# A second set of expert weight buffers, loaded a trip ahead, and a step's wait for the pieces of the bias

## The reference

```
def _L0_ffn_ref(x, ...):
    x = x + _msa(_layernorm(x, ln1_w, ln1_b), w_qkv, w_proj)     # softmax attention
    x = x + _moe_mlp(_layernorm(x, ln2_w, ln2_b), gate_w, gate_b, w1, w2)
    return x
# _moe_mlp: expert = argmax(x @ gate_w + gate_b) of 8, then gelu(x @ w1[expert]) @ w2[expert]
x = L0_attn_x
x = x + 0.5 * _L0_ffn_ref(_layernorm(x), ...)                    # stage 0
x = x + _L0_attn_ref(_layernorm(x), ..., rel_bias_table)         # stage 1, scores + relative bias
x = x + 0.5 * _L0_ffn_ref(_layernorm(x), ...)                    # stage 2
```

## Time and profile before

| | us |
|---|---|
| median of 3 runs | 2681.46 (2679.43 to 2685.08) |
| the profiled execution | 2694.05, span 2692.2 |
| PE busy | 2393.4 (89%) |
| ACT, DVE, POOL busy | 2023.6 (75%), 1966.4 (73%), 807.2 (30%) |
| mean granted clock of PE | 0.945 of full speed |
| DMA | 257.55 MB, 96 GB/s |
| copy of the turned tokens on ACT (L1182) | 0.67 each |
| the 24 matmuls of a trip's w1 product | 2.94 at full clock, 4.30 to 5.46 in the tail |
| mean granted clock in the trips of the tail | 0.77 to 0.80 |
| issues of two scatters in a row on POOL | 1.26 apart |
| POOL's gather of batch 2 in the tail, last issue | 2619.5 to 2621.0 |
| POOL's gather, first of the last eight | starts at 2672.32, eight end at 2686.8 |

### The profile page before, as it was taken

One profiled execution on the slowest core, in us unless ns is written; L12 is line 12 of the kernel. 1 busy time (PEld: TensorE's weight loads), 2 busy tenths in 40 slices (PEclk: granted clock), 3 DMA queues, 4 the chain that ended last, 5 costly groups with the idle time before them and its releaser, 6 DMA issues.

```text
span 2692.2 us, 63549 instructions
## 1 busy us (share of the span) xinstructions
PE 2393.4 (89%) x24940; PEld 947.9 (35%) x24940; DVE 1966.4 (73%) x3256; ACT 2023.6 (75%) x3724; POOL 807.2 (30%) x1087
## 2 busy tenths in 40 slices
PE   3899987888998999999999999999998998998824
PEld 1232323323533543443333333332223432533524
DVE  6988993687588579668888888898987697597000
ACT  1688875777788778777777777888988887888711
POOL 1353432443243151224333113114121033043051
PEclk7899998989999999999999999999999999999957
DMA  4333245534324542643533423211103304303324
GB/s 110 98 109 111 64 118 157 141 86 114 104 61 99 168 141 89 174 129 96 150 104 97 141 81 104 61 26 38 50 17 86 105 14 104 104 14 75 99 54 132
DMA packets 259826, 257.55 MB, mean 96 GB/s; under 512 B 48860, under 2 KB 216604, under 8 KB 255400
## 3 DMA queue, kind: packets, MB, share of 16 engines
q1 hardware_dynamic: 248264, 245.10, 31.5%
q0 software_dynamic: 11264, 8.40, 1.8%
HBM read 189.54 MB, written 76.15 MB: 99 GB/s over the span
## 4 chain that ended last, share of the span: by engine, by line
PE 54%; DVE 16%; ACT 7%; issue 7%; DMA 6%; SPq 6%; POOL 3%; POOLq 0%; DVEq 0%; ACTq 0%
PE psum L905 18%; DVE maxes L1209 12%; PE psum L832 10%; PE psum L867 8%; PE psum L888 4%; ACT probs L1092 4%; PE psum L1040 4%; DMA neg_max<-max_parts 3%; PE psum L1029 3%; PE psum L848 2%; SPq L468 2%; PE psum L956 2%; ACT L1092 2%; DMA q_staged<-neg_max 1%; DVE biased L1214 1%
## 5 line engine op out<-in xcount | busy, mean ns | idle before, releaser
L1092 ACT ACTIVATE probs<-psum 128x512 f32<-128x512 f32 x3072 | 1659.5, 598 | 320.3 <-PE psum L867 182.3
L1209 DVE TENSOR_REDUCE maxes<-psum 128x2 f32<-128x1024 f32 x1216 | 1435.4, 1218 | 394.6 <-PE psum L832 392.2
L905 PE MATMUL psum<-probs,v_ones 128*9 128x256 f32 (+1 forms) x11520 | 947.5, 401 | 0.0
L867 PE MATMUL psum<-q_staged,k_staged 51*128 51x512 bf16 (+1 forms) x3072 | 638.9, 384 | 62.5 <-ACT probs L1092 41.0
L832 PE MATMUL psum<-k_staged,q_staged 48*128 48x512 bf16 x3072 | 612.8, 395 | 78.9 <-DVE maxes L1209 50.0
L1214 DVE CUSTOM_DVE_ANT_0 biased<-psum,strips 128x512 bf16<-128x512 f32 x640 | 413.0, 687 | 113.7 <-PE psum L832 101.4
L644 POOL CAST max_parts<-max_turned 128x32 bf16<-128x32 f32 x96 | 20.1, 209 | 1318.9 <-DVE max_turned L1252 1318.9
L832 PEld LDWEIGHTS psum<-k_staged,q_staged 48*128 48x128 bf16 x3072 | 147.8, 93 | 725.2 <-DVE maxes L1209 364.2
L867 PEld LDWEIGHTS psum<-q_staged,k_staged 51*128 51x128 bf16 (+1 forms) x3072 | 258.5, 95 | 216.3 <-ACT probs L1092 96.6
L905 PEld LDWEIGHTS psum<-probs,v_ones 128*9 128x9 f32 x11520 | 171.1, 88 | 395.5 <-issue 282.5
L1029 PE MATMUL psum<-m_yt,m_w 128*128 128x128 f32 x960 | 133.7, 303 | 22.7 <-DMA m_w<-in_w 22.3
(11 more groups left out here) (143 smaller groups left out, 1571.7 us busy)
## 6 DMA issues: line engine op xcount, KB each, us to landing
m_w<-in_w SPq DMA_DIRECT2D x240, 256.0 KB, 3.4
near<-bias_near SPq DMA_DIRECT2D x16, 1920.0 KB, 9.7
q_staged<-q_parts SPq DMA_DIRECT2D x96, 192.0 KB
k_staged<-k_parts SPq DMA_DIRECT2D x96, 192.0 KB
strips<-bias_strips SPq DMA_DIRECT2D x16, 1152.0 KB, 5.6
q_parts<-p_part SPq DMA_DIRECT2D x24, 384.0 KB, 3.2
k_parts<-p_part SPq DMA_DIRECT2D x24, 384.0 KB, 3.8
bias_cuts<-bias_window SPq DMA_DIRECT2D x64, 120.0 KB
```

Source lines behind the costliest of these rows:

```text
L867: mm_ = pe.matmul(bank[:, :], k.kst[p][rows_, j // 2, kt * P:(kt + 1) * P], k.qst[p][rows_, j // 2, half * HALF:(half + 1) * HALF], start= ...
L905: last = pe.matmul(heads_bank[32 * j:32 * j + VC, columns], k.v[:, batch_of(u) * KT + kt, u % QUADS * 4 + j, :], probs[:, step % 3 * 4 + j ...
L1092: act.activation(probs[:, step % 3 * 4 + e % 4, :], bank[:, :], ACT.Exp).then_inc(taken, 1)
L1209: dve.reduce_max(maxes[u % 2][:, half, 2 * i:2 * i + 2, t, chunk], slot, AX.X).then_inc(drained, 1)
```

## The change

The weights get two sets of buffers, used by the parity of the trip's number over all sets, each with its own pair of semaphores. A load of a set of buffers waits for the trip two before, not for the last one. On SP, the weights of trips 0 and 1 of a set are loaded at `route_step` + 13 to + 16 (w1 of trip 0, w2 of trip 0, w1 of trip 1, w2 of trip 1, one a step), those of trip t + 2 in the steps after trip t's w1 product. The first tokens are loaded at the trip's step - 4 in place of - 2, which is a step ahead of the `carry_max`. The store of a trip's result now stands ahead of a w2 load. The room that the descriptors of POOL's DMAs get is set to 4096 bytes a partition. And in all steps in which pieces of the bias are handled, SP waits, before anything of `sp_between`, for the first score tile of that step.

```diff
@@ -258,7 +258,8 @@
     route_chain = k.sem("route_chain")
     scattered = [k.sem(f"scattered{p}") for p in range(2)]
     gathered = [k.sem(f"gathered{p}") for p in range(2)]
-    m_in, w1_in, w2_in, m_stored, finished = (k.sem(s) for s in ("m_in", "w1_in", "w2_in", "m_stored", "finished"))
+    m_in, m_stored, finished = (k.sem(s) for s in ("m_in", "m_stored", "finished"))
+    w1_in, w2_in = [k.sem(f"w1_in{p}") for p in range(2)], [k.sem(f"w2_in{p}") for p in range(2)]
 
 
     probs = k.sb("probs", [P, 3 * 4, HALF])
@@ -330,8 +331,8 @@
     numbers, upto = k.sb("tile_numbers", [P, MT]), k.sb("upto", [P, E * E])
     y = k.sb("m_y", [P, SLOTS, C])
     y_t = k.sb("m_yt", [P, SLOTS * P])
-    w1 = [k.sb(f"m_w1_{r}", [P, HID]) for r in range(SLOTS)]
-    w2 = [k.sb(f"m_w2_{r}", [P, 4, C]) for r in range(SLOTS)]
+    w1 = [[k.sb(f"m_w1_{p}_{r}", [P, HID]) for r in range(SLOTS)] for p in range(2)]
+    w2 = [[k.sb(f"m_w2_{p}_{r}", [P, 4, C]) for r in range(SLOTS)] for p in range(2)]
     hidden = [k.sb(f"m_hidden{r}", [P, HID]) for r in range(SLOTS)]
     expert_out = k.sb("m_out", [P, SLOTS, C])
 
@@ -356,6 +357,12 @@
 
     def batch_of(u):
         return u // QUADS % B
+
+    def trip_index(n, b, trip):
+        return set_index[n, b] * TRIPS + trip
+
+    def trip_key(done):
+        return (*SETS[done // TRIPS], done % TRIPS)
 
     def group_tiles(b, h):
         return slice(b * KT + h * 4, b * KT + h * 4 + 4)
@@ -539,25 +546,24 @@
 
     def load_w1(sp, n, b, trip):
 
-        at = set_index[n, b]
-        sp.wait_ge(routed, at + 1)
-        if at or trip:
-            before = (n, b, trip - 1) if trip else (*SETS[at - 1], TRIPS - 1)
-            sp.wait_ge(taken, seat[("m_hidden", *before, SLOTS - 1)] + 1)
+
+        done = trip_index(n, b, trip)
+        sp.wait_ge(routed, set_index[n, b] + 1)
+        if done >= 2:
+            sp.wait_ge(taken, seat[("m_hidden", *trip_key(done - 2), SLOTS - 1)] + 1)
         for r in range(SLOTS):
-            sp.dma_start(w1[r][:, :], w["ffn"]["w1"][bass.ds(expert_of(sp, n, b, trip, r), 1), :, :].rearrange(
-                "o p h -> p (o h)")).then_inc(w1_in, 16)
+            sp.dma_start(w1[done % 2][r][:, :], w["ffn"]["w1"][bass.ds(expert_of(sp, n, b, trip, r), 1), :, :].rearrange(
+                "o p h -> p (o h)")).then_inc(w1_in[done % 2], 16)
 
     def load_w2(sp, n, b, trip):
 
-        at = set_index[n, b]
-        sp.wait_ge(routed, at + 1)
-        if at or trip:
-            before = (n, b, trip - 1) if trip else (*SETS[at - 1], TRIPS - 1)
-            sp.wait_ge(taken, seat[("m_down", *before)] + 1)
+        done = trip_index(n, b, trip)
+        sp.wait_ge(routed, set_index[n, b] + 1)
+        if done >= 2:
+            sp.wait_ge(taken, seat[("m_down", *trip_key(done - 2))] + 1)
         for r in range(SLOTS):
-            sp.dma_start(w2[r][:, :, :], w["ffn"]["w2"][bass.ds(expert_of(sp, n, b, trip, r), 1), :, :].rearrange(
-                "o (q p) c -> p (o q) c", p=P)).then_inc(w2_in, 16)
+            sp.dma_start(w2[done % 2][r][:, :, :], w["ffn"]["w2"][bass.ds(expert_of(sp, n, b, trip, r), 1), :, :].rearrange(
+                "o (q p) c -> p (o q) c", p=P)).then_inc(w2_in[done % 2], 16)
 
     def store_tokens(sp, n, b, trip):
 
@@ -573,6 +579,9 @@
 
     def sp_between(sp, step):
 
+        cutting = any(-1 - CUT_LOADS <= step - s < 15 for s in NEAR_STEPS)
+        if cutting or step // 8 * len(QUIET) < QUADS * (CUTS + STRIP_CUTS):
+            sp.wait_ge(scored, seat["exp", step // UNIT_STEPS, step % UNIT_STEPS * 4] + 1)
         if step % 8 in QUIET:
             piece = step // 8 * len(QUIET) + QUIET.index(step % 8)
             if piece == 0:
@@ -594,18 +603,23 @@
                 store_parts(sp, n, b, h)
         for n, b in SETS:
             first = trip_step(n, b, 0)
-            if step == first - 2:
+            for trip in range(2):
+                if step == route_step(n, b) + 13 + 2 * trip:
+                    load_w1(sp, n, b, trip)
+                if step == route_step(n, b) + 14 + 2 * trip:
+                    load_w2(sp, n, b, trip)
+            if step == first - 4:
                 load_tokens(sp, n, b, 0)
-                load_w1(sp, n, b, 0)
-                load_w2(sp, n, b, 0)
             for trip in range(TRIPS):
-                if step == trip_step(n, b, trip) + 2 and trip + 1 < TRIPS:
-                    load_tokens(sp, n, b, trip + 1)
-                    load_w1(sp, n, b, trip + 1)
+                if step == trip_step(n, b, trip) + 2:
+                    if trip + 1 < TRIPS:
+                        load_tokens(sp, n, b, trip + 1)
+                    if trip + 2 < TRIPS:
+                        load_w1(sp, n, b, trip + 2)
                 if step == trip_step(n, b, trip) + 3:
-                    if trip + 1 < TRIPS:
-                        load_w2(sp, n, b, trip + 1)
                     store_tokens(sp, n, b, trip)
+                    if trip + 2 < TRIPS:
+                        load_w2(sp, n, b, trip + 2)
         for b in range(B):
             if step == gather_step(2, b) + 4:
                 store_batch(sp, b)
@@ -1021,23 +1035,23 @@
 
     def pe_hidden(pe, n, b, trip, r):
 
-        bank = open_bank(pe, "m_hidden", n, b, trip, r)
+        bank, done = open_bank(pe, "m_hidden", n, b, trip, r), trip_index(n, b, trip)
         if r == 0:
             pe.wait_ge(taken, seat["m_turn", n, b, trip] + 1)
-            pe.wait_ge(w1_in, (set_index[n, b] * TRIPS + trip + 1) * SLOTS * 16)
+            pe.wait_ge(w1_in[done % 2], (done // 2 + 1) * SLOTS * 16)
         for q in range(4):
-            last = pe.matmul(bank[:, q * P:(q + 1) * P], w1[r][:, q * P:(q + 1) * P], y_t[:, r * P:(r + 1) * P],
+            last = pe.matmul(bank[:, q * P:(q + 1) * P], w1[done % 2][r][:, q * P:(q + 1) * P], y_t[:, r * P:(r + 1) * P],
                              start=True, stop=True)
         last.then_inc(scored, 1)
 
     def pe_down(pe, n, b, trip):
 
-        bank = open_bank(pe, "m_down", n, b, trip)
-        pe.wait_ge(w2_in, (set_index[n, b] * TRIPS + trip + 1) * SLOTS * 16)
+        bank, done = open_bank(pe, "m_down", n, b, trip), trip_index(n, b, trip)
+        pe.wait_ge(w2_in[done % 2], (done // 2 + 1) * SLOTS * 16)
         for r in range(SLOTS):
             pe.wait_ge(taken, seat["m_hidden", n, b, trip, r] + 1)
             for q in range(4):
-                last = pe.matmul(bank[:, r * P:(r + 1) * P], hidden[r][:, q * P:(q + 1) * P], w2[r][:, q, :],
+                last = pe.matmul(bank[:, r * P:(r + 1) * P], hidden[r][:, q * P:(q + 1) * P], w2[done % 2][r][:, q, :],
                                  start=q == 0, stop=q == 3)
         last.then_inc(scored, 1)
 
@@ -1654,7 +1668,7 @@
         "upto": np.tril(np.ones((E, E), np.float32)).reshape(-1),
         "numbers": np.arange(MT).astype(np.float32),
     }
-    nc = bacc.Bacc("TRN2", target_bir_lowering=False, num_devices=1)
+    nc = bacc.Bacc("TRN2", target_bir_lowering=False, num_devices=1, dynamic_dma_scratch_size=4096)
     ins = {name: nc.dram_tensor(f"in_{name}", v.shape, F32, kind="ExternalInput").ap() for name, v in arrays.items()}
     out = nc.dram_tensor("out", (B, N, C), F32, kind="ExternalOutput").ap()
     w = {
```

## The result

The changed kernel took 2655.14 us (median of 4 runs, 2647.52 to 2657.57) against 2681.31 for the kernel before in the same session: ratio 0.9896, 95% interval 0.9873 to 0.9919. Two more comparisons of the same kernel gave 0.9876 (0.9858 to 0.9895) and 0.9904 (0.9882 to 0.9927). The forecast was 2653 in 2638 to 2673. The profiled execution took 2657.57 us (span 2655.7) at a mean granted clock of 0.952, against 2694.05 at 0.945.

The account below looks back on a forecast made before the run. PE, 89% busy, was taken to set the time, so transfers win only where PE stands still. Terms -13.9 - 8 - 1 + 3 + 1 - 12 + 2.5 = -28.4 us took the median from 2681.46 to 2653, range 2638 to 2673.

Parts of the forecast that it names:

- Where the gaps are: PE's waits in the earlier profile: 60.9 us for tokens (`m_y`), 22.3 for weights (`m_w`), ten places each.
- Part 1, the four first turns: First token turns of four sets: idle -13.9 us gone, slow clock -8 of 12.9 at stake.
- Batch 1: Stage 0's batch 1 set: gap of 3 to 5 us nearly eaten by `carry_max` coming 3.6 late; -1 us.
- First set: SP, already 9 us late to the maxima, gets 6.9 us more issues ahead: +3 us, ends -2 and +8.
- The pieces' waits and the rest: Attention: spreading bias pieces delays projection stores, +2.5 us (-3 to +10); weights ahead of trip 0's `carry_max`, +1 over seven sets.
- Part 2, the tail: Weight waits -15.6 us, first tokens +1.8 later, tokens behind the output store +2 once: -12, ends -8 and -19.
- The room for descriptors: POOL's DMAs: the smaller descriptor room costs 0, since two or three are ever in flight.
- The signs: Profile after: `m_w` under 4 us, `m_y` about 20, clock 1.00 in stage 2, tail w1 products 9 us apart.
- A: Only the tail gains; the body's token waits become `carry_max` waits: -9 us, or 2672; chance 0.16.
- B: Every removed gap keeps the clock up, in body and tail: 40 us gained, or 2641; chance 0.09.
- C: Slower: twelve loads make both `carry_max` of a set late where SP lacks idle time: +40, or 2721; chance 0.09.
- D: Spread bias pieces cost the full step everywhere, +16 in place of +2.5 us: -15, or 2666; chance 0.07.

Follow-up runs that it names:

- tokens early only: Kernel before, with only the first tokens of a set loaded at the trip's step - 4 in place of - 2: 2687.38 us, ratio 1.0017.
- tail reordered: Changed kernel; last set's second-trip weights behind its first tokens, later w2 loads behind their trip's tokens, output stores of batches 0 to 2 16 steps later: 2643.75 us.
- tokens late: Changed kernel with the first tokens of a set back at the trip's step - 2, behind `carry_max`: 2678.99 us, ratio 0.9984.
- reordered kernel: Changed kernel; every set's trip 1 weights behind first tokens and `carry_max`, later w2 loads behind their trip's tokens, no waits for bias pieces: 2650.94 us.
- small room: Kernel before, with only the room for POOL's DMA descriptors set to 4096 bytes a partition: 2685.08 us, ratio 0.9998.

## Why the prediction was right, step by step

*Where the gaps are.* Right: the waits of the earlier trace rows were the main part of the gain.

*Part 1, the four first turns.* -13.9 and -8 for the clock, -21.9 together; the table shows -24.1. The turns wait for nothing, the clock is 1.00 at all four, and 10 (by the table) to 12 us (by the stretches behind the turns) of the 12.9 at stake came back where 8 was taken. But the prediction put this to the tokens and called the weights' waits the smaller matter, "inside the attention 3 us are left". The run with the tokens early only shows what it overlooked: there the weights are what is late next, by 4.2 to 4.9 us at five places. The number was right because the change moves both, not for the reason given.

*Batch 1.* -1 forecast. The mechanism is as forecast: one gap turned into another. The table's -0.7 can't be told from nothing, since executions of one kind differ by 3 us there.

*First set.* +3 forecast, on the reasoning that SP is 9 us late already and gets 6.9 more. It got 8.0 more (9.0 to 17.1). The wait ends 5.2 us later than before (420.54 against 415.31), but it also begins 2.6 later (402.56 against 399.94). "The tokens come earlier and help nothing" is wrong: they are issued no earlier, and of the 5.2 us 4.7 are in their transfer, 7.2 us in place of 2.5. Steps 96 to 112 take 6.4 us longer (means of three), the next 16 steps 4.6 less, and the stretch stands at +2.7, with the pieces' waits in it. So the size is near by a mechanism that is half the one forecast.

*The pieces' waits and the rest.* The waits' +2.5 was too large: alone they gave -2.6 (-5.9 to +0.5). That `carry_max` of trip 0 and the queue cost +1 elsewhere isn't seen; the other steps gained 3.4. The sum left out the 3 us of waits for weights inside the attention, which are gone now. That the 3.4 are these is not shown: with the tokens early only, and the weights late, the same steps took 1321.4, less than in the changed kernel.

*Part 2, the tail.* This is the term that was mis-sized: -12 forecast, -6.9 measured. Its gain was right (19.34 us of waits for weights against 4.15 for ACT's copy: -15.2, where -15.6 stood). The two prices against it were too low. The first tokens came 3.8 us later after routing, not 1.8: from the cast of the routing's result (2595.19 before, 2565.25 after) the issue is at 12.3 and 14.1 us, the 1.8 forecast, and the turn at 14.9 and 18.7. The other 2.0 are in the transfer. It landed 2.5 us after its issue before, when SP had issued nothing for some time, and 4.5 us right behind the weights. The second price, 2 us once behind the store of `out`, was 4.19 and 3.16 at two trips. The first of these is as forecast in its cause (the store, a `w2` trio and then the tokens), but the price comes again at the fifth trip without that store: the tokens of the fourth and fifth trips are issued 7.9 and 10.2 us behind those of the trip before, and PE needs 6.9 us for a trip at full clock. That made 15.2 - 3.8 - 7.35 = 4 us, and a clock of 0.81 in place of 0.77 the other 3, for which the sum had nothing: PE is busy 33.4 us for the trips in place of 36.5. With the tail reordered the three waits are back at 18.54 and nothing, though 0.76 and 2.02 for `m_out` come up in their place, and it gains 10 us.

Here the rule bears on it that the prediction had weighed only for `carry_max`. The Trainium skill ("DMA: Bandwidth & Descriptors", section "Queues, rings and completion order") has each DMA engine take the descriptors of a ring in their order; by that, a small transfer queues behind large ones issued before it. The 2.5 and 4.5 us agree with it, and so do the 2.5 and 7.2 of the first set. That it is the order and not the shared bandwidth is not shown by any run here.

*The room for descriptors.* 0 forecast, -0.02% (-0.16 to +0.11%) measured.

*The signs.* The row for `m_w` is gone, the clock is 1.00, the w1 products of the tail are 9.7 us apart (9 forecast), and SP came to the maxima of the first set 17.1 us late (over 10). One sign failed: the row for `m_y` was to fall from 60.9 to about 20, and it is 57.4. 17.98 of it are the first set, whose tokens were thought to be early, 6.80 a later trip of that set (5.14 before), 7.35 the third and fifth trips of the tail.

*The total.* 2653 against 2655.14 is closer than the terms are. The tail missed by 5 us one way; the four turns (2 us), the first set with the pieces' waits (3) and the other steps (4) missed the other way. That these nearly cancel is luck.

*Rivals.* A (only the tail gains) falls by the table; tokens late is what A would have looked like, at 2679. B's clock came near in the body and not in the tail. C's lateness came in the first set and in batch 1, where SP had no idle time, and nowhere else, as its condition said. D's full step isn't seen.

## What to carry to other kernels

When two transfers that one step needs stand behind the same queue entry, moving one of them ahead bought nothing here: ask for each what is late next, and move both or none. On a queue that issues in order, put what is wanted soonest first, and a store that waits for another engine last, above all in a tail where nothing covers a wait. A row of total waits can stay the same (60.9 to 57.4) while the places that matter change; read the places.

## What the runs showed of the hardware

- After an idle of 2.02 us, the turn and another 0.81, PE's next w1 product took 5.46 us in place of 2.92 (in the reordered kernel 4.54 after 1.66); after idle times of 0.76, 0.81 and 0.86 it stayed at 2.92 (reordered tail). In the first trip of stage 2 an idle of 0.80 left the clock at 1.00. 
- The same transfer of tokens landed 2.5 us after issue with SP idle ahead of it, 3.4 to 4.5 right behind three to twelve weight loads, 7.2 behind the pieces of the bias (first set), and 10.9 behind loads of 1.9 MB of bias rows (second trip of stage 0, batch 2, in the changed kernel). What shares of it are order and bandwidth no run shows.
- Two executions of programs alike in the body (before, and small room) differed by 9 us (2455.3 against 2446.1 from first to last step), nearly all at two places (62.7 against 56.7 in steps 96 to 112, 74.6 against 70.6 in 240 to 256). A gain of a few us at one place needs several profiles.
